# Relative attention: queries' loads on a semaphore of their own, band products that wait for those alone

## The reference, cut to what matters

```
scores = einsum('bhid,bhjd->bhij', Q, K) / sqrt(8)
idx    = clip(r[None, :] - r[:, None], -64, 64) + 64
scores = scores + einsum('bhid,ijd->bhij', Q, rel_k_emb[idx])
attn   = softmax(scores)
context = einsum('bhij,bhjd->bhid', attn, V) + einsum('bhij,ijd->bhid', attn, rel_v_emb[idx])
```

## Time and profile before

| | us |
|---|---|
| median of 3 runs (1837.62 to 1852.1) | 1840.69 |
| the profiled execution | 1835.92 |
| its span | 1834.1 |
| layer 1's attention, from its first band products to the last division | 272 to 839 |

### The profile page before, as it was taken

One profiled execution on the slowest core, in us unless ns is written; L12 is line 12 of the kernel. 1 busy time (PEld: TensorE's weight loads), 2 busy tenths in 40 slices (PEclk: granted clock), 3 DMA queues, 4 the chain that ended last, 5 costly groups with the idle time before them and its releaser, 6 DMA issues. The chain is left out here.

```text
span 1834.1 us, 32772 instructions
## 1 busy us (share of the span) xinstructions
PE 1523.2 (83%) x12067; PEld 733.9 (40%) x12067; DVE 1168.7 (64%) x2509; ACT 914.5 (50%) x1755; POOL 473.3 (26%) x408
## 2 busy tenths in 40 slices
PE   5989744998888888988748988889848988889998
PEld 4656422434433433334313434344323343344443
DVE  4323667745855855834668988635658988617777
ACT  1332232666656666665225666642224666555453
POOL 0701437756756756730210000000020000000000
PEclk9989865999999999999768999899868999789999
DMA  7232257666766666730240100022170010004332
GB/s 216 84 94 73 58 164 185 181 160 172 179 160 164 178 169 168 183 84 1 75 148 20 37 20 20 2 73 90 33 225 20 20 37 20 2 6 111 100 98 80
DMA packets 218198, 179.13 MB, mean 98 GB/s; under 512 B 57600, under 2 KB 186136, under 8 KB 217624
## 3 DMA queue, kind: packets, MB, share of 16 engines
q1 hardware_dynamic: 207928, 160.34, 32.4%
q10 hardware_dynamic: 8064, 12.51, 2.4%
q0 software_dynamic: 2048, 4.20, 0.8%
HBM read 108.64 MB, written 67.64 MB: 96 GB/s over the span
## 5 line engine op out<-in xcount | busy, mean ns | idle before, releaser
L1924 DVE TENSOR_REDUCE a1a_partial<-a1a_room 128x4 f32<-128x1024 f32 x192 | 226.4, 1221 | 30.8 <-PE a1a_room L1989 30.2
L2365 ACT ACTIVATE a3a_probsT<-a3a_st 128x512 f32<-128x512 f32 (+2 forms) x320 | 155.7, 560 | 123.5 <-PE a3a_st L2431 73.6
L1883 ACT ACTIVATE a1a_probsT<-a1a_st 128x512 f32<-128x512 f32 (+1 forms) x416 | 204.7, 575 | 13.9 <-PE a1a_st L2022 12.6
L2365 ACT ACTIVATE a2a_probsT<-a2a_st 128x512 f32<-128x512 f32 (+2 forms) x320 | 155.6, 560 | 111.1 <-PE a2a_st L2431 65.8
L2276 DVE TENSOR_REDUCE a3a_maxima<-a3a_room 128x2 f32<-128x1024 f32 (+3 forms) x160 | 170.2, 1113 | 34.5 <-PE a3a_room L2400 23.7
L2276 DVE TENSOR_REDUCE a2a_maxima<-a2a_room 128x2 f32<-128x1024 f32 (+3 forms) x160 | 170.2, 1113 | 25.6 <-PE a2a_room L2400 19.2
L1788 POOL TENSOR_TENSOR a1a_shifted<-a1a_shifted,a1a_best 128x1024 f32<-128x1024 f32 x64 | 121.7, 1903 | 93.5 <-DVE a1a_best L1930 67.2
L1920 DVE CUSTOM_DVE_ANT_0 a1a_shifted<-a1a_room,a1a_bands 128x256 f32<-128x256 f32 x256 | 93.3, 421 | 75.4 <-PE a1a_room L1989 67.4
L2059 PE MATMUL a1a_ctx<-a1a_probsT,a1a_vpad 128*9 128x512 f32 (+3 forms) x1408 | 139.3, 494 | 0.8
L1989 PE MATMUL a1a_room<-stack 48*128 48x128 bf16 (+1 forms) x1376 | 108.2, 261 | 37.1 <-DVE a1a_partial L1924 19.0
L2022 PE MATMUL a1a_st<-stack 51*128 51x512 bf16 (+3 forms) x576 | 116.7, 317 | 19.7 <-ACT a1a_nearT L1890 6.2
(11 more groups left out here) (464 smaller groups left out, 3092.1 us busy)
## 6 DMA issues: line engine op xcount, KB each, us to landing
a1a_bands<-a_band SPq DMA_DIRECT2D x112, 192.0 KB, 3.8
a_near<-a1a_shifted SPq DMA_DIRECT2D x112, 192.0 KB, 3.1
a1a_near<-a_near SPq DMA_DIRECT2D x64, 256.0 KB, 4.0
f_rows<-l_gates SPq DMA_DIRECT2D x64, 256.0 KB, 3.0
a_band<-a1a_r_mix SPq DMA_DIRECT2D x64, 254.0 KB, 3.5
stack<-q SPq DMA_DIRECT2D x96, 96.0 KB
f_rows<-l_gates SPq DMA_DIRECT2D x64, 128.0 KB, 3.0
stack<-k SPq DMA_DIRECT2D x32, 96.0 KB
```

The lines of the kernel that those rows point to most:

```text
L1883: nc.scalar.activation(dst, src, ACT.Exp).then_inc(exp_done, 1)
L1924: nc.vector.tensor_reduce(partial[:, g % 2, :, 1 + r].rearrange("p (a s) -> p a s", a=2), src, X_AXIS, ALU.max).then_inc(job_free, 1)
L2365: nc.scalar.activation(probsT[:, block_at % BLOCK_ROOMS, place:place + heads, lo:], src, ACT.Exp).then_inc(exp_done, 1)
```

## The change

The queries' transfers signal a new semaphore, `asked[U % 2]`, those of the keys still `stacked[U % 2]`. (The sets of unit 0 are loaded in the stage before, all on `stacked[0]`; the two count functions take care of that.) The first band job of a unit waits for `asked`; the first near or far max job of a unit waits for `stacked`. The model of `work_order` gets a time for each: band jobs of a unit are due 6 us (`q_time`) after the last far step of the unit two before it, all other jobs after 14 us as they were.

```diff
-    LOADS = 16 * 2 * (2 * len(queries.pieces) + sum(len(s.pieces) for s in keys))
+    Q_LOADS, K_LOADS = 16 * 2 * 2 * len(queries.pieces), 16 * 2 * sum(len(s.pieces) for s in keys)
...
+    def asked_count(U):
+        return Q_LOADS * (U // SETS + (1 if U % SETS else 0))
+    def stacked_count(U):
+        return K_LOADS * (U // SETS + 1) + (0 if U % SETS else Q_LOADS)
...
+        asked_at = {U: 4000.0 + (U - 1) * load_time + q_time for U in range(SETS)}
...
-                    job_at = max(job_at, stack_at.get(g // TILES, 1e12))
+                    job_at = max(job_at, (asked_at if what == "band" else stack_at).get(g // TILES, 1e12))
...
-                        stack_at[V // 2 + SETS] = now + load_time
+                        stack_at[V // 2 + SETS], asked_at[V // 2 + SETS] = now + load_time, now + q_time
...
+    first_job = {}
+    for event in jobs:
+        if event[0] in ("near max", "far max"):
+            first_job.setdefault(event[1] // TILES, event)
...
+        asked = [ph.sem(f"asked{n}") for n in range(SETS)]
...
-                    for s, src in enumerate([queries] + keys):
-                        src.load(sp, stack[U % SETS][s], i, b, stacked[U % SETS])
+                    queries.load(sp, stack[U % SETS][0], i, b, asked[U % SETS])
+                    for s, src in enumerate(keys):
+                        src.load(sp, stack[U % SETS][1 + s], i, b, stacked[U % SETS])
...
-                        if what == "band" and I == 0:
-                            pe.wait_ge(stacked[U % SETS], LOADS * (U // SETS + 1))
+                        if what == "band" and I == 0 and asked_count(U):
+                            pe.wait_ge(asked[U % SETS], asked_count(U))
+                        if what == "band" and n == 0 or event == first_job[U]:
+                            pe.wait_ge(stacked[U % SETS], stacked_count(U))
```

More of the change, by code:

```diff
@@ L1523, in work_order @@
     def work_order():
-        latency, rows_in_dma, load_time, switch, split_time, copy_time = 250.0, 8000.0, 14000.0, 60.0, 1300.0, 1600.0
+        latency, rows_in_dma, load_time, q_time, switch, split_time, copy_time = 250.0, 8000.0, 14000.0, 6000.0, 60.0, 1300.0, 1600.0
         order, now, wide = [], 0.0, False
@@ L1853, in _ @@
                 for n in range(SETS):
-                    sp.wait_ge(stacked[n], LOADS * len(range(n, UNITS, SETS)))
+                    U = max(range(n, UNITS, SETS))
+                    sp.wait_ge(asked[n], asked_count(U))
+                    sp.wait_ge(stacked[n], stacked_count(U))
             @block.scalar
```

## The result

1825.84 us in the median of 6 runs (1822.33 to 1829.17), against 1845.65 for the kernel before on the same chip: a ratio of 0.9892 (0.9868 to 0.9916). The forecast was 1821. The profiled execution took 1826.68, with a span of 1824.8 us. In it the stage ends, with its last division, at 821.30 in place of 838.47: 17.17 us sooner, where the sum had 17.8. The steps of that sum came out otherwise, though, and it was luck that they cancelled.

A forecast was written before the change was run, and what follows sets the result against it. TensorE, busy 83% of the span, was taken to bound the kernel. Removing 21.7 us of waits less 3.9 of new ones gave 17.8, so 1835.9 became 1818.1; 3 added for the median made 1821, range 1808 to 1839.

The forecast's parts named there:

- Removed, 21.7 us: At unit boundaries, TensorE's five waits for the right keys, 15.0 us of waiting, go and take 21.7 us with them.
- two falls of the clock in second halves: Second halves of the fourth and sixth periods, 2.54 us longer together; not counted as cost of the boundary waits.
- the larger gain: Rival: no wait at all, both second-half clock falls gone, shorter eight-tile stretches; about 30 us gained, 1809; chance 0.08.
- TensorE at F + 5.3, SP on time: TensorE reaches the moved band job 5.3 us after F, the boundary's last far steps' end; SP issues queries on time.
- When are the queries in?: Queries land at F + 5.9, taking a 4.6 us landing; 0.6 us of wait at six boundaries, 3.9 us in all.
- Given back elsewhere, nothing: VectorE's first pass, a 49.6 us stretch of eight tiles, might limit the period; counted as nothing, 1 us a period either way.
- The two bounds, 63.2 and 63.4: Period by VectorE's unshortened eight-tile stretch, 63.2 us, and by the period without a wait plus the new wait, 63.4.
- Clock at 1.00 behind each boundary: Sign: TensorE's granted clock is 1.00 in the 10 us behind each of the six boundaries.
- The signs that it named: Profile after: keys' wait gone, query waits 0 to 1.2 us, issues within 1 us of F, clock 1.00, divisions 62 to 64 apart.
- SP late: Rival: SP stays 5.2 us late at boundaries, 5.8 us waits for queries; 31 us slower, about 1870; chance 0.09.
- The smaller wait: Rival: query waits of 1.5 us or more, a boundary costing 2 to 2.5; about 1830, no change; chance 0.33.
- That the queries come as late as the keys: Rival: queries' signal as late as the keys', 4.3 us wait, 39 us in all, 17 slower; counted in the slower case.

The follow-up runs named there:

- the semaphore alone: Against the kernel before: the band job waits for the queries alone, but the planner counts 14 us for them, so every engine's order stays the old one; ratio 0.9865.
- the order alone: The change's order, but a unit's first band job waits for queries and keys, as in the kernel before; ratio to before 1.0014.
- before again: The unchanged kernel before, profiled a second time, one execution; its stage ended at 844.4 us and the rest took 1007.2 us.
- the run at 8 us: The change with 8 in place of 6 us for the queries in the planner, so the band job stands later; 1818.06 us, ratio to before 0.9855.

## Why the prediction was right, point by point

- *Removed, 21.7 us.* Right: with the semaphore alone the six periods are 399.8 - 378.3 = 21.5 us shorter, and five of them, at 62.8, equal the one period without a wait from which the price was read. (A fall of the clock that is new in the first period, and one that is gone from the fourth, cancel here.) Of the "two falls of the clock in second halves", on which the larger gain counted, the one in the fourth period is in the trace of before (0.72 over 636 to 642 us); in the sixth period's second half the clock was 1.00 (752 to 784 us), so its 1.2 us are something else.
- *TensorE at F + 5.3, SP on time.* Right to 0.1 us, and to 0 to 1.1 us.
- *When are the queries in?* This term was too small: 0.6 us of wait at each boundary, measured 1.2 to 2.9, 1.9 on average (11.3 in all for 3.9). The landing taken, 4.6 us, was even above the median one (4.0 to 4.5). But a median landing was added to the last issue: at the first boundary that gives 377.45 + 3/4 x 1.74 + 4.1 = 382.9, and the band job began at 384.06. It waits for the last of the four, and that one took 5.2 us there and 5.1 on average. The trace of before had such a number in the row that was used: the last of the near tiles' loads took 5.1.

```profile
a1a_near<-a_near SPq DMA_DIRECT2D x1, 256.0 KB, 5.1
```

  Of the 1.3 us that were missing at a boundary the last one's landing is 0.5 and SP's lateness another 0.5; the rest is a slower issue of the four and the step from landing to band job. With the near tiles behind the queries both big parts are gone, so their place ahead in the queue is shown to be the main cause of the waits.
- *Given back elsewhere, nothing.* Wrong to the other side. The two bounds, 63.2 and 63.4, agreed because both came from the old order's rows; the stretch of eight tiles became 1.3 us shorter, more than the 1 us a period left for it. The prediction had named the possibility and put it at nothing.
- *Clock at 1.00 behind each boundary.* Four of six in one execution, six of six in the other.
- *The signs that it named.* Three of them failed: waits of 0 to 1.2 us on the queries (one was 2.93, over the 2.4 that "would make it wrong"), the clock at 1.00, and odd divisions 62 to 64 us apart (62.3 to 65.5). The wait for the keys is gone, and SP's lateness is 1.1 us at most, as forecast but for 0.1.
- *The rivals.* SP late: refuted. The smaller wait: its waits came in full, and the shorter periods paid for most of them, so the time lies between its 1830 and the forecast. That the queries come as late as the keys: the order alone shows what that would have been.
- *The time.* The sum was meant for an execution like the profiled one. There the stage gained 17.2, but the rest took 7.9 us longer (1003.5 for 995.6) in code that is the same. In these twelve executions it took 994.5 to 1007.3, and 995.6 and 1007.2 in the two of the kernel before: it varies so without the change, and with the clock that is granted in it, 0.91 and 0.89 in those two. The first line is before, the second before again:

```profile
838.47:1834.06 995.59, 846.04 (x6386) 384.10 (x6386) 691.00 (x1263) 488.28 (x921) 37.23 (x38) 0.91 0.20 57
```

```profile
844.42:1851.55 1007.13, 860.04 (x6386) 390.43 (x6386) 690.88 (x1263) 488.50 (x921) 37.25 (x38) 0.89 0.20 56
```

  By medians the gain is 19.8 us, and 1844.4 - 1817.24 = 27.2 when the change was measured again, where the sum had 17.8. The 3 us added for the median were too few: the kernel before came to 1845.65, 9.7 above its profiled execution. So the removed waits are why the time fell, as predicted; that it fell by about as much as forecast is luck, since a wait three times too short and a shorter way that was left out came to nearly the same.

## What to carry to other kernels

Splitting a wait by what each consumer needs brought here as much with the consumer left in place (0.9865) as with it moved up to the new signal (0.9863), because the move bought a new wait; the moved order paid only when that wait was taken away too (0.979). When a transfer becomes the one that is waited for, try to move its issue ahead of the others in the queue, and price it by the last transfer that the wait needs, not by the median: here the last came 2.0 to 2.3 us sooner behind the first issue, on average, with the near tiles moved behind the queries. And read a price over a period, not from a wait alone, since the way between waits changes with the order.

## What the runs showed of the hardware

- The length of a wait did not tell whether the clock would fall: it did after 1.89 and 2.35 us and not after 2.93 in one execution, not after 1.73 to 1.89 in another, and in the run at 8 us behind a wait of 0.53, to 0.57 (the band job stands at 505.73 there):

```profile
508.00:512.00 4.00, 4.00 (x26) 1.23 (x24) 3.12 (x3) 1.25 (x4) 1.12 (x1) 0.57 0.36 81
```

Falls also came where no load was waited for at the band job: in the change at 420 to 424 us (0.58), and in before again at 553 to 557 (0.57); in the 4 us ahead of that TensorE's longest wait was 0.3 us, and the clock 1.00. So the fall behind 0.53 us need not be that wait's. The Trainium skill (TensorE: Matmul & The Clock Gate, section "HAM oscillation — how this bites in real kernels") lets a fall follow gaps in which TensorE waits for transfers between bursts of matmuls; the trace agrees for all six waits of 4.5 to 6.4 us with the order alone; in the change for two of six in one execution and none of six in the other.
- A 96 KB load on the same queue took 2.6 us to land ahead of 768 KB, and 4.2 behind it (medians of four at the second boundary); the last of the four took 2.7 and 5.7.
